# Rows normalised while they are centred, the bias added by TensorE, and a unit's sums divided on ScalarE in a graph attention kernel

## The chip, the core and the metric

The kernel runs on one core of a Trainium2 chip. The metric is device time in microseconds (us), the median of several runs. A core has TensorE (PE in the profile), VectorE (DVE), ScalarE (ACT), GpSimd (POOL) and SyncE (SP), each with its own instruction stream; they meet at semaphores. Transfers are issued by SyncE and GpSimd.

## What is computed

One graph attention layer over 8192 nodes, with rows of 256 numbers, a dense 8192 x 8192 matrix of edge weights of which few are above zero, and 8 heads of 32:

```python
h = relu((x - mean(x)) / sqrt(var(x) + 1e-5))
hw = (h @ W.T).reshape(n, 8, 32)
attn = s_src[:, None, :] + s_dst[None, :, :]      # (hw * a_src).sum(-1), (hw * a_dst).sum(-1)
attn = attn + adj[:, :, None] * We[:, 0] + be
attn = leaky_relu(where(adj[:, :, None] > 0, attn, -inf), 0.2)
attn = softmax(attn, axis=1)
out = x + einsum('ijh,jhd->ihd', attn, hw).reshape(n, 256) + h @ Wr.T + br
```

## The kernel before

**First stage.** 32 units of 256 rows. VectorE takes mean and variance of a unit (L731, L735) and the negated mean (L738). ScalarE centres and rectifies (`centre`, L1150), takes the standard deviation (`deviation`, L1154), copies the turned rows out of PSUM (`turned`, L1158) and later the projections (`copies`, L1168), scaled by one over the deviation, which VectorE makes with a reciprocal (`scales`, L743). Since the rectifier passes a positive factor, that factor is applied only behind the projections. TensorE turns the rows (`turn`, L1309) and projects them (`maps`): features and scores (L1323), and the residual `h @ Wr.T` (L1326). VectorE's `add_biases` adds `be` to the scores (L748) and makes residual times factor plus x (L753). GpSimd writes the features to a table in DRAM (L594), adds `br` to the residual (L596) and writes it to the output and to a spare copy (L600, L601). SyncE loads x into four buffers (L481). Beside this work VectorE searches the window lists: the first rows of the matrix, which have the most edges, cut into four groups of windows (L783, L772, and sorting with L841, L843). At the end the lists are ranked by length: `count` and `place` on VectorE with TensorE's sums between, ending in the ranks (L901).

**Second stage.** 67 units of 128 list rows each. Groups of lists are dealt in the order of their ranks by GpSimd (`deal`, L651) and read back (`load_dealt`, L663). For a unit of K list places GpSimd issues K gathers (L626), each of one table row per partition, into a ring of 86 slots. VectorE adds the gathered scores, applies the leaky rectifier, takes the row maximum and subtracts it (L918, L922, L926, L929). ScalarE prepares the next unit's edge terms (L1192), takes the exponentials (L1209) and weights the last two fifths of the places, head by head (L1215); VectorE weights the others (L939). TensorE sums over the places (L1347 and L1353). VectorE's `evacuate` then takes the reciprocal of the summed weights (L948) and multiplies (L952), and GpSimd adds the rows to the output four units later (L642). Between, VectorE searches the matrix rows of later units: 63 searches; one or two per unit up to unit 45, from there on one in about every second unit, and none after unit 60.

**What sets the order.** Each engine's order is written out. VectorE's unit loop is: search, then sorting steps that alternate with the four score steps, then weighting, decoding of the found list, and `evacuate` of the unit before. ScalarE's loop is: `prepare(u + 1)`, then `exps(u)`. The profile's tile names are coarse: "arena" holds the ring, the lists and all the first stage's buffers; "banks" is PSUM; "w_all" and "more_out" hold the finished rows.

## Time and profile before

| | us |
|---|---|
| median of 3 runs | 2311.83 |
| lowest and highest | 2309.43, 2316.55 |
| the profiled execution | 2312.84 |
| its span, first to last instruction | 2310.8 |

Every count of busy time and every wait is of the profiled execution. A wait is put down to what ended it. Busy shares hide which stretch an engine bounds, so the waits and the stretches are read beside them.

### The profile page before, as it was taken

How to read it: one execution, taken by the hardware profiler on the slowest of the kernel's cores; microseconds unless marked ns; L12 is line 12 of the kernel's file. 1: busy time of each engine (PE TensorE's matmuls, PEld its weight loads, DVE VectorE, ACT ScalarE, POOL GpSimd, SP SyncE). 2: the span in 40 equal slices, each digit the busy share in tenths (PEclk: the TensorE clock that was granted, in tenths of full speed). 3: DMA queues.
4: the chain of work that ended last, by engine and by line, in shares of the span. 5: the costliest groups of instructions: out<-in, count | busy, mean ns of one | idle time of the engine just before them, and what ended most of it. 6: DMA issues, size and time to landing. Idle time of an engine off the chain costs nothing. (4 is left out here: it accounts for less than half of the span.)

```text
span 2310.8 us, 22965 instructions
## 1 busy us (share of the span) xinstructions
PE 1002.1 (43%) x3773; PEld 789.3 (34%) x3774; DVE 2024.3 (88%) x5351; ACT 1115.5 (48%) x4803; POOL 1595.9 (69%) x2020
## 2 busy tenths in 40 slices
PE   4767304522453194236332643353253336363343
PEld 3555203322432173225321532242242225242232
DVE  5899797899699789999888999999999998887942
ACT  2333205633574384446543654545354446485553
POOL 5544476777776777677777777777677774777775
PEclk9998656766675667667765766666666667676676
DMA  6444876667466757877777777777778885667333
GB/s 148 161 148 138 290 229 160 200 213 236 131 212 213 223 159 235 251 236 228 219 218 222 225 254 229 249 250 247 247 256 242 257 249 174 203 197 217 88 76 65
DMA packets 164570, 473.62 MB, mean 205 GB/s; under 512 B 35888, under 2 KB 54360, under 8 KB 164216
## 3 DMA queue, kind: packets, MB, share of 16 engines
q1 hardware_dynamic: 86088, 278.11, 36.6%
q0 software_dynamic: 78336, 194.09, 30.6%
q14 instruction: 118, 0.97, 0.1%
q8 instruction: 28, 0.46, 0.1%
HBM read 435.24 MB, written 36.83 MB: 204 GB/s over the span
## 5 line engine op out<-in xcount | busy, mean ns | idle before, releaser
L626 POOL DMA_INDIRECT arena<-table,arena x1262 | 1270.7, 1007 | 479.2 <-issue 322.1
L1347 PE MATMUL banks<-arena,ident 128*128 128x264 f32 x1566 | 500.2, 492 | 1161.9 <-DVE arena L939 1161.9
L1215 ACT ACTIVATE arena<-arena 128x32 f32<-128x32 f32 x3832 | 819.3, 307 | 2.2
L1347 PEld LDWEIGHTS banks<-arena,ident 128*128 128x128 f32 x1566 | 385.0, 251 | 1273.7 <-issue 1050.9
L772 DVE FIND_INDEX8 work<-work,adj_sb 128x8 uint32<-128x502 f32 (+56 forms) x775 | 667.2, 865 | 0.0
L783 DVE MAX8 work<-adj_sb 128x8 f32<-128x502 f32 (+56 forms) x775 | 652.4, 856 | 0.0
L1209 ACT ACTIVATE arena<-pre 128x104 f32<-128x104 f32 (+22 forms) x81 | 23.3, 304 | 910.1 <-DVE pre L929 909.6
L1353 PE MATMUL banks<-arena,ident 128*128 128x264 f32 x958 | 254.4, 408 | 42.5 <-ACT arena L1215 42.5
L939 DVE TENSOR_TENSOR arena<-arena 128x1024 f32<-128x1024 f32 (+8 forms) x169 | 226.4, 1389 | 51.3 <-ACT arena L1209 51.2
L1353 PEld LDWEIGHTS banks<-arena,ident 128*128 128x128 f32 x958 | 181.7, 197 | 103.6 <-ACT arena L1215 76.2
L1192 ACT ACTIVATE pre<-arena,we_all 128x13 f32<-128x13 f32 (+26 forms) x536 | 165.3, 406 | 87.3 <-DMA arena<-lists 87.0
L918 DVE TENSOR_TENSOR pre<-pre,arena 128x104 f32<-128x104 f32 (+22 forms) x81 | 21.4, 279 | 139.2 <-DMA arena<-table,arena 129.0
L841 DVE MAX8 work<-work 128x8 f32<-128x56 f32 (+11 forms) x536 | 122.5, 270 | 2.4
L843 DVE MATCH_REPLACE8 work<-work 128x56 f32<-128x56 f32 (+11 forms) x402 | 106.6, 273 | 0.0
L642 POOL DMA_INDIRECT out_dram<-w_all,arena x41 | 66.7, 1626 | 50.2 <-DVE w_all L952 27.3
L1150 ACT ACTIVATE arena<-arena 128x256 f32<-128x256 f32 x64 | 29.0, 500 | 138.2 <-DVE arena L738 138.2
L651 POOL DMA_INDIRECT lists<-arena,rank x67 | 67.9, 1014 | 30.0 <-issue 25.0
L1323 PE MATMUL banks<-w_all,arena 128*128 128x272 f32 x256 | 83.2, 454 | 1.9 <-ACT arena L1158 1.8
L1369 PE MATMUL banks<-work,ones 128*128 128x24 f32 (+9 forms) x390 | 73.5, 336 | 0.0
L1326 PE MATMUL banks<-w_all,arena 128*128 128x256 f32 x256 | 72.3, 408 | 0.0
L596 POOL TENSOR_TENSOR arena<-arena 128x512 f32<-128x512 f32 x32 | 40.5, 1265 | 44.5 <-DVE arena L753 44.0
L1369 PEld LDWEIGHTS banks<-work,ones 128*128 128x128 f32 x390 | 69.2, 264 | 0.0
(130 smaller groups left out, 966.2 us busy)
## 6 DMA issues: line engine op xcount, KB each, us to landing
adj_sb<-in_adj_dram SPq DMA_DIRECT2D x505, 512.0 KB, 4.4
arena<-table,arena POOLq DMA_INDIRECT x1262, 3.8
table<-arena POOLq DMA_DIRECT2D x32, 264.0 KB, 2.7
arena<-in_x_dram SPq DMA_DIRECT2D x32, 256.0 KB, 2.9
resid<-arena POOLq DMA_DIRECT2D x32, 256.0 KB, 2.6
out_dram<-arena POOLq DMA_DIRECT2D x32, 256.0 KB, 2.8
adj_sb<-in_adj_dram SPq DMA_DIRECT2D x1, 1536.0 KB, 23.5
lists<-arena,rank POOLq DMA_INDIRECT x67, 3.9
```

Source lines behind the costliest of these rows:

```text
L626: pool.indirect_dma_start(gath[0:n, un.slot(k), :], None, table[:, :], bass.IndirectOffsetOnAxis(ap=rec[0:n, k, 0:1], axis=0)).then_inc(la ...
L772: v.max_index(idx8[:, 8 * s:8 * s + 8], val8[:, 8 * s:8 * s + 8], a[:, bounds[s]:bounds[s + 1]]).then_inc(S["scanned"], 1)
L783: v.max(val8[:, 8 * s:8 * s + 8], a[:, bounds[s]:bounds[s + 1]]).then_inc(S["maxed"], 1)
L841: v.max(top, keys_of).then_inc(done, 1)
L843: v.match_replace(keys_of, top, keys_of, 0.0).then_inc(done, 1)
L939: last = v.tensor_tensor(gv, gv, pb.unsqueeze(3).to_broadcast([P, n, H, D]), ALU.mult)
L1192: last = s.activation(pv[:, h, :], pairs(rec, K)[:, :, 1], ACT.Identity, scale=we_all[:, h:h + 1], bias=rec[:, 1 + h:2 + h])
L1215: last = s.activation(g, g, ACT.Copy, scale=gath[:, un.slot(k), HD + h:HD + h + 1])
L1323: m.matmul(ps_hd[:, q, b, :], rows, w_all[:, c, 0:272], start=(c == 0), stop=(c == 1))
L1347: last = m.matmul(ps_sum[:, u % 2, :], ident[:, :], gath[:, un.slot(k), :], start=(k == 0), stop=False)
L1353: last = m.matmul(ps_sum[:, u % 2, :], ident[:, :], gath[:, un.slot(k), :], start=False, stop=(k == K - 1))
L1369: m.matmul(rv[:, i, :], ones[:, :], same[:, j * D:(j + 1) * D], start=False, stop=(i == n - 1 and j == i - 1))
```

## The change

**First stage.** VectorE no longer negates the mean at once. One unit later, once ScalarE has the deviation, it takes the reciprocal and makes minus mean times reciprocal, and ScalarE normalises in the same instruction that rectifies. The projections then need no factor: ScalarE copies a unit's two blocks in one instruction, and VectorE adds residual and x in one instruction. `br` comes from TensorE, as a product of a row of ones and the row of `br`, accumulated with the residual. `add_biases` follows three units behind instead of two; x has eight buffers instead of four. GpSimd waits for its output writes after it has dealt and loaded the window lists, not before.

**Second stage.** VectorE keeps the reciprocal (`invert`), now between the score steps of the next unit and its weighting. The multiplication is on ScalarE, one instruction per head, between the exponentials and the weighting of the next unit.

```diff
-        x_sb = part(4 * 2 * IN).rearrange("p (u b n) -> p u b n", u=4, b=2)
+        x_sb = part(8 * 2 * IN).rearrange("p (u b n) -> p u b n", u=8, b=2)
...
-                    nc.gpsimd.tensor_tensor(rt_sb[:, q, :, :], rt_sb[:, q, :, :],
-                                            br_all.unsqueeze(1).to_broadcast([P, 2, HD]), ALU.add
-                                            ).then_inc(S["br_added"], 1)
-                    pool.wait_ge(S["br_added"], u + 1)
...
-            for b in range(2):
-                for q, each in (("hd_out", 16), ("res_out", 32)):
-                    pool.wait_ge(S[f"{q}{b}"], each * (UNITS // 2))
-
-            pool.wait_ge(S["pad_out"], 16)
...
             deal(groups[0])
             load_dealt(groups[0])
+            for b in range(2):
+                for q, each in (("hd_out", 16), ("res_out", 32)):
+                    pool.wait_ge(S[f"{q}{b}"], each * (UNITS // 2))
+            pool.wait_ge(S["pad_out"], 16)
...
-                dve.wait_ge(S["mv_done"], u + 1)
-                v.tensor_scalar(nmean[:, q, :], mv[:, q, :, 0], -1.0, None, ALU.mult).then_inc(S["nmean_done"], 1)
...
+                v.scalar_tensor_tensor(out=nmean[:, q, :], in0=mv[:, q, :, 0], scalar=-1.0, in1=rstd[:, q, :],
+                                       op0=ALU.mult, op1=ALU.mult).then_inc(S["nmean_done"], 1)
...
-                for b in range(2):
-                    last = v.scalar_tensor_tensor(out=rt_sb[:, q % 2, b, :], in0=ps_res[:, q % 2, b, :],
-                                                  scalar=rstd[:, q, b:b + 1], in1=x_sb[:, q, b, :],
-                                                  op0=ALU.mult, op1=ALU.add)
-                last.then_inc(S["res_done"], 1)
+                v.tensor_tensor(rt_sb[:, q % 2, :, :], ps_res[:, q % 2, :, :], x_sb[:, u % 8, :, :], ALU.add
+                                ).then_inc(S["res_done"], 1)
...
-            def evacuate(un):
+            def invert(un):
...
-                v.tensor_tensor(out_sb[u % OUTS].rearrange("p (h d) -> p h d", d=D),
-                                ps_sum[:, u % 2, 0:HD].rearrange("p (h d) -> p h d", d=D),
-                                rinv[:, u % 2, :].unsqueeze(2).to_broadcast([P, H, D]), ALU.mult).then_inc(S["evac"], 1)
...
+                    if m == 4 and un.u:
+                        invert(units[un.u - 1])
...
+                if u:
+                    evacuate(units[u - 1])
                 act.wait_ge(S["exped"], u + 1)
...
+            def evacuate(un):
+
+                u = un.u
+                act.wait_ge(S["recip"], u + 1)
+                if u >= OUTS:
+                    landed(act, units[u - OUTS].store_seq + (2 if units[u - OUTS].partial else 1))
+                for h in range(H):
+                    last = s.activation(out_sb[u % OUTS][:, h * D:(h + 1) * D], ps_sum[:, u % 2, h * D:(h + 1) * D],
+                                        ACT.Copy, scale=rinv[:, u % 2, h:h + 1])
+                last.then_inc(S["evac"], 1)
...
+                m.matmul(ps_res[:, q, :, :], ones[0:1, :], br_all[0:1, :].unsqueeze(1).to_broadcast([1, 2, HD]),
+                         start=True, stop=False)
```

Line numbers of the changed kernel differ; the names tell what is what. On TensorE, the last unit of the first stage and the ranks behind it, before:

```order
L1323 MATMUL banks<-w_all,arena 128x272 x2
L1326 MATMUL banks<-w_all,arena 128x256 x2
L1323 MATMUL banks<-w_all,arena 128x272 x2
L1326 MATMUL banks<-w_all,arena 128x256 x2
L1364 MATMUL banks<-above_sum,ones 128x61
```

The same place in the changed kernel:

```order
L1323 MATMUL banks<-arena,ones 128x512
L1328 MATMUL banks<-w_all,arena 128x272 x2
L1331 MATMUL banks<-w_all,arena 128x256 x2
L1328 MATMUL banks<-w_all,arena 128x272 x2
L1331 MATMUL banks<-w_all,arena 128x256 x2
L1370 MATMUL banks<-above_sum,ones 128x61
```

The product for `br` stands ahead of each unit's eight others, 32 times in all. On ScalarE, from the exponentials of unit 48 (128x9x8) to the weighting of unit 49, before:

```order
L1209 ACTIVATE arena<-pre 128x9x8
L1215 ACTIVATE arena<-arena 128x32 x24
L1192 ACTIVATE pre<-arena,we_all 128x7 x8
L1199 ACTIVATE pre<-ones 32x16
L1199 ACTIVATE pre<-ones 32x8
L1209 ACTIVATE arena<-pre 128x8x8
L1215 ACTIVATE arena<-arena 128x32 x24
```

The same place in the changed kernel, with the division of units 47 and 48 at L1215:

```order
L1197 ACTIVATE arena<-pre 128x9x8
L1215 ACTIVATE more_out<-banks,rinv 128x32 x8
L1205 ACTIVATE arena<-arena 128x32 x24
L1180 ACTIVATE pre<-arena,we_all 128x7 x8
L1187 ACTIVATE pre<-ones 32x16
L1187 ACTIVATE pre<-ones 32x8
L1197 ACTIVATE arena<-pre 128x8x8
L1215 ACTIVATE w_all<-banks,rinv 128x32 x8
L1205 ACTIVATE arena<-arena 128x32 x24
```

Eight instructions stand between a unit's exponentials and its weighting, ahead of everything that ScalarE does for the next unit. On VectorE, the end of unit 48 and the start of unit 49, before:

```order
L929 TENSOR_TENSOR pre<-pre,rmax 128x72
L841 MAX work<-work 128x8 x2
L834 TENSOR_SCALAR ahi<-work 128x20
L939 TENSOR_TENSOR arena<-arena 128x3x256 x2
L855 TENSOR_SCALAR arena<-work 128x20
L856 SCALAR_TENSOR_TENSOR arena<-work,ahi 128x20
L860 TENSOR_TENSOR flags<-flag,work 128x1
L948 RECIPROCAL rinv<-banks 128x8
L952 TENSOR_TENSOR more_out<-banks,rinv 128x256
L918 TENSOR_TENSOR pre<-pre,arena 128x64
```

The same place in the changed kernel:

```order
L920 TENSOR_TENSOR pre<-pre,rmax 128x72
L832 MAX work<-work 128x8 x2
L939 RECIPROCAL rinv<-banks 128x8
L825 TENSOR_SCALAR ahi<-work 128x20
L930 TENSOR_TENSOR arena<-arena 128x3x256 x2
L846 TENSOR_SCALAR arena<-work 128x20
L847 SCALAR_TENSOR_TENSOR arena<-work,ahi 128x20
L851 TENSOR_TENSOR flags<-flag,work 128x1
L909 TENSOR_TENSOR pre<-pre,arena 128x64
```

The reciprocal has moved ahead of the weighting (L939 before, L930 now), behind the score step that releases ScalarE, and the multiplication is gone.

## Rows read from the trace of the kernel before

**Rows 1.** the page, part 1: busy us, share of the span, instructions

```profile
PE 1002.1 (43%) x3773; PEld 789.3 (34%) x3774; DVE 2024.3 (88%) x5351; ACT 1115.5 (48%) x4803; POOL 1595.9 (69%) x2020
```

**Rows 2.** waits of VectorE, whole run: us in total, times, longest

```profile
DVE pre L918 <- DMA arena<-table,arena: 129.0, 16, 18.9
DVE arena L939 <- ACT arena L1209: 51.2, 16, 9.4
DVE arena L731 <- DMA arena<-in_x_dram: 10.1, 2, 5.1
DVE s_all L748 <- ACT arena L1168: 9.6, 9, 3.1
```

**Rows 3.** busy times by stretch: length, busy us per engine, granted clock, DMA

```profile
27.00:234.00 207.00, 147.00 (x578) 112.66 (x579) 182.07 (x929) 70.08 (x177) 94.37 (x110) 0.89 0.51 153
234.00:257.00 23.00, 17.99 (x89) 14.54 (x87) 11.29 (x37) 6.87 (x17) 16.45 (x19) 0.94 0.93 336
...
1477.00:1942.00 465.00, 198.27 (x752) 161.41 (x752) 459.44 (x971) 223.00 (x984) 324.95 (x316) 0.66 0.79 247
```

**Rows 4.** groups of VectorE instructions, 0-400 us: busy us, mean ns

```profile
L753 DVE SCALAR_TENSOR_TENSOR arena<-banks,arena 128x256 f32<-128x256 f32 x64 | 27.8, 476 | 1.0 <-DMA out_dram<-arena 1.0
...
L738 DVE TENSOR_SCALAR arena<-arena 128x2 f32<-128x2 f32 x32 | 9.3, 290 | 1.1
```

**Rows 5.** timeline inside the first stage: start us, us, engine, line, operation

```profile
120.23 0.76 DVE L731 BATCH_NORM_STATS2 arena<-arena 128x6 f32<-128x256 f32 x2
...
121.30 0.53 DVE L738 TENSOR_SCALAR arena<-arena 128x2 f32<-128x2 f32 x1
...
122.83 0.66 PE L1309 MATMUL banks<-ident,arena 128*128 128x128 f32 x4 [0.61 <-ACT arena L1150]
...
125.58 0.76 DVE L731 BATCH_NORM_STATS2 arena<-arena 128x6 f32<-128x256 f32 x2
...
126.30 1.03 PE L1326 MATMUL banks<-w_all,arena 128*128 128x256 f32 x4
...
138.30 0.17 DVE L738 TENSOR_SCALAR arena<-arena 128x2 f32<-128x2 f32 x1
```

**Rows 6.** the loads of x (L481): us from issue to landing

```profile
DMA to landing us min/median/max: 2.5/2.9/10.3
```

**Rows 7.** timeline of VectorE, then of GpSimd, from the window lists' ranks on

```profile
256.80 0.17 DVE L901 CAST rank<-rank_f 128x4 uint32<-128x4 f32 x1
...
264.50 1.08 POOL L651 DMA_INDIRECT lists<-arena,rank  x1 [7.71 <-issue]
...
272.85 0.80 POOL L663 DMA_DIRECT2D arena<-lists  x1 [3.46 <-DMA lists<-arena,rank]
281.11 1.15 POOL L626 DMA_INDIRECT arena<-table,arena  x1 [7.46 <-DMA arena<-lists]
```

**Rows 8.** waits of VectorE between 1942 and 2160 us

```profile
DVE arena L939 <- ACT arena L1209: 34.7, 8, 5.9
```

**Rows 9.** timeline of units 60 and 61, to the last group's deal

```profile
2190.66 6.89 ACT L1215 ACTIVATE arena<-arena 128x32 f32<-128x32 f32 x32
...
2192.92 0.20 DVE L948 RECIPROCAL rinv<-banks 128x8 f32<-128x8 f32 x1
...
2193.59 0.16 DVE L874 COPY arena<-ids 128x4 uint32<-128x4 uint32 x1
...
2204.30 0.42 DVE L901 CAST rank<-rank_f 128x4 uint32<-128x4 f32 x1
...
2206.40 0.99 POOL L651 DMA_INDIRECT lists<-arena,rank  x1 [1.14 <-DMA arena<-table,arena]
```

**Rows 10.** waits of ScalarE, then of GpSimd, whole run

```profile
ACT arena L1209 <- DVE pre L929: 909.6, 57, 84.1
...
POOL arena L626 <- PE banks L1353: 0.3, 1, 0.3
```

**Rows 11.** timeline at the end of the last unit

```profile
2293.81 0.42 DVE L952 TENSOR_TENSOR w_all<-banks,rinv 128x256 f32<-128x256 f32 x1
```

More of the change, by code:

```diff
@@ L478, in load_x @@
             def load_x(u):
[L479 to L481 removed]
+                if u >= 8:
+                    sp.wait_ge(S["x_free"], u - 7)
+                sp.dma_start(x_sb[:, u % 8, :, :], by_unit(x, u)).then_inc(S[f"x_in{u % 8}"], 16)
             for u in range(4):
@@ L727, in normalize @@
             def normalize(u, q):
-                dve.wait_ge(S[f"x_in{q}"], 16 * (u // 4) + 16)
+                dve.wait_ge(S[f"x_in{u % 8}"], 16 * (u // 8) + 16)
                 for b in range(2):
-                    last = v.bn_stats(stat[:, q, b, :], x_sb[:, q, b, :])
+                    last = v.bn_stats(stat[:, q, b, :], x_sb[:, u % 8, b, :])
                 last.then_inc(S["bn_done"], 1)
@@ L948, in evacuate @@
                 v.reciprocal(rinv[:, u % 2, :], ps_sum[:, u % 2, HD:ROW]).then_inc(S["recip"], 1)
-                if u >= OUTS:
-                    landed(dve, units[u - OUTS].store_seq + (2 if units[u - OUTS].partial else 1))
-                dve.wait_ge(S["recip"], u + 1)
-                v.tensor_tensor(out_sb[u % OUTS].rearrange("p (h d) -> p h d", d=D),
-                                ps_sum[:, u % 2, 0:HD].rearrange("p (h d) -> p h d", d=D),
-                                rinv[:, u % 2, :].unsqueeze(2).to_broadcast([P, H, D]), ALU.mult).then_inc(S["evac"], 1)
             def combine_clear():
@@ L1011, in _ @@
                 normalize(u, u % 4)
+                if u:
+                    scales(u - 1, (u - 1) % 4)
                 windows_beside(u)
-                scales(u, u % 4)
-                if u >= 2:
-                    add_biases(u - 2, (u - 2) % 4)
+                if u >= 3:
+                    add_biases(u - 3, (u - 3) % 4)
+            scales(UNITS - 1, 3)
+            count(groups[0])
+            add_biases(UNITS - 3, 1)
             add_biases(UNITS - 2, 2)
-            count(groups[0])
             add_biases(UNITS - 1, 3)
@@ L1042, in _ @@
                     done_finds += 1
-                if un.u:
-                    evacuate(units[un.u - 1])
                 for group in groups[1:]:
@@ L1055, in _ @@
                     combine_out()
-            evacuate(units[-1])
+            invert(units[-1])
             dve.wait_ge(S["fl_t"], 1)
@@ L1149, in centre @@
                 for b in range(2):
-                    last = s.activation(hn[:, q % 2, b, :], x_sb[:, q, b, :], ACT.Relu, bias=nmean[:, q, b:b + 1])
+                    last = s.activation(hn[:, q % 2, b, :], x_sb[:, u % 8, b, :], ACT.Relu, bias=nmean[:, q, b:b + 1],
+                                        scale=rstd[:, q, b:b + 1])
                 last.then_inc(S["hn_done"], 1)
             def deviation(u, q):
+                act.wait_ge(S["mv_done"], u + 1)
                 s.activation(sdev[:, q, :], mv[:, q, :, 1], ACT.Sqrt, bias=eps[:, :]).then_inc(S["sd_done"], 1)
@@ L1165, in copies @@
                     act.wait_ge(S["s_done"], u - 1)
-                act.wait_ge(S["rstd_done"], u + 1)
-                for b in range(2):
-                    last = s.activation(hd_sb[:, q % 2, b, :], ps_hd[:, q % 2, b, :], ACT.Copy,
-                                        scale=rstd[:, q, b:b + 1])
-                last.then_inc(S["hd_copied"], 1)
+                s.activation(hd_sb[:, q % 2, :, :], ps_hd[:, q % 2, :, :], ACT.Copy).then_inc(S["hd_copied"], 1)
+            deviation(0, 0)
             for u in range(UNITS):
+                if u + 1 < UNITS:
+                    deviation(u + 1, (u + 1) % 4)
                 centre(u, u % 4)
-                deviation(u, u % 4)
                 if u:
@@ L1225, in _ @@
                     s.activation(comb_w, comb_w, ACT.Exp).then_inc(S["comb_exp"], 1)
+            evacuate(units[-1])
             done = act.alloc_register("dense_act")
@@ L1302, in _ @@
             pe.wait_ge(S["wt_copied"], 2)
+            pe.wait_ge(S["small_in"], 48)
             def turn(u, q):
@@ L1325, in maps @@
                         rows = hnT[:, q, b, c * P:(c + 1) * P]
-                        last = m.matmul(ps_res[:, q, b, :], rows, w_all[:, c, 272:528], start=(c == 0), stop=(c == 1))
+                        last = m.matmul(ps_res[:, q, b, :], rows, w_all[:, c, 272:528], start=False,
+                                        stop=(b == 1 and c == 1))
                 last.then_inc(S["proj_done"], 1)
```

10 lines of the change are left out of this document (4 added, 6 removed).

## The prediction

> **What bounds the kernel now.** I read the page's busy shares first: VectorE is busy 88% of the span, ScalarE 48%, GpSimd 69% [rows 1]. A mean like that hides changes of regime, so the next views are the waits of VectorE over the whole span and the busy times by stretch. In the waits [rows 2] the reader is to see three releasers: gathered rows that have not landed (129.0 us, 16 times), ScalarE's exponentials (51.2 us, 16 times), and small waits of the first stage. With their places in the timeline they cut the run into five stretches.
>
> *0 to 257 us, the first stage and the ranks of the window lists.* VectorE is busy 182 of 207 us in its main part, TensorE 147 [rows 3]: 6.1 and 4.9 us per unit of 256 rows, thirty units. GpSimd then waits 7.7 us before it deals the window lists, though their ranks are written at 256.97 [rows 7].
>
> *281 to about 1477 us.* Most of the long gather waits lie in here, up to unit 20 at 1294 (the others are at the end); unit 27, another of the units with many places, finds its rows just landed. GpSimd issues gathers nearly without a pause, so this stretch starts and ends with the first gather at 281.11 [rows 7].
>
> *1477 to 1942 us, units 27 to 44.* VectorE is busy 459 of 465 us [rows 3]: every instruction it loses shortens the run.
>
> *1942 to 2160 us.* Units without a search of their own alternate with units that have one. VectorE waits 34.7 us for ScalarE in 8 waits [rows 8]; seven, of 2.6 to 5.9 us, are in units 46, 47, 49, 51, 53, 55 and 57. ScalarE is on the path there: it weights the rows of the unit before, prepares the next, and only then takes the exponentials.
>
> *2160 us to the end.* The last group is dealt as soon as VectorE has ranked it [rows 9], then gathers bound units 63 to 66, then the last unit's chain.
>
> **The change part by part.**
>
> *The wait for the output writes* moves behind the dealing and loading of the window lists. 7.7 us before the first deal become about 0.9, an estimate for the wake-up after a release: -6.8. The writes must still land before the first gather, but that waits longer anyway, for the loaded lists (8 us later, [rows 7]).
>
> *VectorE in the first stage.* Two operations of 476 ns [rows 4], 0.87 us together, become one over 512 elements. None such stands in the trace: it costs 0.87 if nothing is saved, about 0.70 if only a second start is; I take 0.70, since the copies from PSUM grow by about 1 ns per element. The negated mean averages 290 ns, but ran 530 while GpSimd's bias addition ran and 170 otherwise [rows 4, 5]; that addition goes, -0.12. The new order hides one dependency and adds another (the negated mean now waits for the reciprocal), about -0.08. Together -0.37 per unit, -9.6 over units 4 to 29; bounds -5 and -12.
>
> *Loads and waits.* Unit 4 waits 5.1 us for its x, unit 8 another 5.0 (the 10.1 of [rows 2]). With eight buffers x of unit 8 comes in time: -5.0. Unit 4's load is issued some 14 us earlier, but behind the window loads of the same queue; its landing took 10.3 us against a median of 2.9 [rows 6], so it comes little sooner. I take -2 (0 to -4); what is gained before unit 4 is lost in that wait. Short waits for ScalarE, counted in 9.6 us [rows 2], give -1.6 in the middle; the rest lies before unit 4 or in the tail.
>
> *TensorE* gets one product per unit, one row of ones against 512 columns. Two 256-column products beside it take 1.03 us [rows 5] at the granted 2.4 GHz, so it costs 1.03; bounds 0.5 (a single row is cheaper) and 2.1 (the lower clock). A unit took TensorE 4.5 us in [rows 5] (122.83 to 127.33); it will take 5.55. Eight of the units 5 to 29 pass VectorE in 4.7 to 5.3 us, as the 5.35 between the two L731 rows of [rows 5]. With only two buffers between the engines these become TensorE's 5.55 and keep nothing from the long units: +7.4. VectorE reaches unit 30 earlier by 2+5.0+1.6+9.6-7.4 = 10.8.
>
> *The tail of the first stage* grows. The unit behind which centring, turning and projecting run is one deeper, so at unit 30 TensorE owes four projections of 4.9 us instead of three of 3.85, then the ranks. Following the chain, the ranks are done 30.1 us after unit 30 begins, against 22.9 now: +7.2. It counts in full. The first gather moves by -6.8-10.8+7.2 = -10.4.
>
> *281 to 1477*: 0. ScalarE's later weighting frees gather slots later, but a slot is filled again some three units on, and GpSimd waits 0.3 us in the whole run for the sums of ScalarE's part [rows 10]. VectorE's savings end in its waits for gathers.
>
> *The division moved to ScalarE.* VectorE loses the time from 2192.92 to 2193.59, 0.67 us, and pays 0.13 for the reciprocal elsewhere [rows 9]: 18 units times 0.55 = -9.9 in 1477 to 1942 (8.6 to 10.4). The reciprocal comes after the step that releases the exponentials, so they don't wait for it.
>
> On ScalarE eight multiplications of 32 elements go in between exponentials and weighting. The 32 weightings of one unit take 6.89 us [rows 9], 0.215 each, so 1.72; with the reciprocal to wait for, 1.85. Read from PSUM they could cost 2.5 if they behaved like the two-operand forms. In units whose exponentials VectorE does not wait for, this is hidden by ScalarE's idle time: 909.6 us of waiting for VectorE in 57 waits [rows 10]. In the seven units named it is not: 6x1.85+1.7 = 12.8, less seven times the 0.67 that VectorE drops behind the weighting: +8.1. Units 59 and 61 become late in the same way, +2.05-0.65 and +1.55-0.65; 1.4 of slack stands before the deal of the last group [rows 9]. So +9.0; bounds +6 and +14. What is queued behind ScalarE's new wait is its own weighting, then TensorE's sums; GpSimd's stores come four units later and have time.
>
> *The last unit.* Its weighting starts 1.7 later, and its own division is 8 operations, 1.8 us, in place of 0.42 [rows 11]: +3.1.
>
> Here a rule stands against the change. The rows say that ScalarE has room in most units [rows 10] and lacks it in nine. The Trainium skill (ScalarE: Activation LUTs, Rules for kernel authors) would leave multiplications to VectorE rather than ScalarE. By the rule the move would lose wherever it is made; by the rows only where ScalarE is waited for.
>
> **Sum:** -10.4-9.9+9.0+3.1 = -8.2 against the profiled execution's 2312.84 us (2310.8 of span, 2.0 around it): 2304.6. The runs' median is 2311.83, 1.0 lower; on it the sum gives **2304** us, -0.35%. A measurement of this kernel can tell about 0.3%, 6.9 us, from no change.
>
> **The rivals.**
>
> *A larger gain.* The stage's short units cost less because TensorE's product is nearer 0.5 us (+3 in place of +7.4, a tail 2 shorter), and the lists load faster once the writes before them thin out (8 us to landing now, up to -5). For it: the first lists are among the largest and load in the busiest stretch of DMA. Against it: dealing now runs beside those writes. About -18: 2294.
>
> *The gain is eaten.* The divisions cost 2.5 us in the nine waited-for units and the tail is +4.4; the first stage gives only the 6.8 of the wait. Then -6.8-9.9+14+4.4 = +1.7: 2313.
>
> *Slower: TensorE bounds the first stage.* If the product comes at the lower clock (2.1 us) or the unit otherwise takes over 6.9 us, the pace of the thirty units now (207 over 30, [rows 3]), the stage is longer than before. At 7.2, that is 30x0.3 = +9 and +8 more for the tail, with -6.8 for the writes: the first gather is 10 later, and the rest adds -9.9+12.1: +12, 2324. For it: the granted clock is 0.89 of full there now [rows 3]. Against it: TensorE will idle less, and from 234 to 257, where it idles least, the clock is 0.94.
>
> *ScalarE is waited for in every unit.* Its new work then shows in each of the 67: 67x(1.85-0.67) = +79, 2391. The 57 waits [rows 10] speak against it. This is what the rule cited above would make of the move.
>
> *It does not do what it says:* the first stage is no shorter, and only the write wait goes. That is -6.8-9.9+12.1 = -4.6, 2307, inside the forecast's range.
>
> **How the numbers follow.** Forecast (2299 to 2309) 0.42; larger gain 0.18; eaten 0.26; slower 0.13; ScalarE in every unit 0.01. The threshold, 2304.9, halves the forecast and leaves the larger gain whole: faster 0.21+0.18 and a part of luck in the eaten case, 0.43; same 0.42; slower 0.15. The range reaches from the larger gain to the middle of the slower case: 2292 to 2318. The forecast's own is 2299 to 2309.
>
> **What would show it.** In the profile after: the first gather near 271; TensorE's units in the first stage 5.5 us apart where they were 4.7 to 5.3, and four of them back to back at its end; no bias addition on GpSimd, and a negated mean near 170 ns; VectorE's waits for exponentials up from 51 to about 65 us with the same nine units; 18 units between 1477 and 1942 shorter by 0.55 each; first-list deal within 1 us of the ranks. Wrong would be a first gather later than 278 or before 262, ScalarE's eight divisions over 2.2 us, or a wait of VectorE on the sums at the reciprocal's new place.

## The result: 0.9% faster, more than forecast

The changed kernel takes 2295.82 us (median of 7 runs, 2288.58 to 2297.49); the kernel before, on the same chip, 2316.55 us (7 runs, 2309.43 to 2324.84). The ratio is 0.9909, with a 95% interval of 0.9893 to 0.9925. That is 21 us, where the forecast had 8. Its sign was right and the time lies in the stated range, but it lies outside the forecast's own range, next to the rival that was called a larger gain.

The profiled execution of the changed kernel has a span of 2295.8 us against 2310.8. The page's busy shares, which answer to [rows 1]:

```profile
PE 1064.3 (46%) x3837; PEld 806.6 (35%) x3838; DVE 1980.8 (86%) x5252; ACT 1205.9 (53%) x5306; POOL 1551.3 (68%) x1988
```

VectorE lost 43.5 us of work, ScalarE gained 90, GpSimd lost its 40 us of additions, TensorE gained 62. The waits of VectorE over the whole span, which answer to [rows 2] (us in total, times, longest):

```profile
DVE pre L909 <- DMA arena<-table,arena: 142.6, 17, 20.0
DVE rinv L939 <- PE banks L1359: 47.7, 10, 5.9
DVE s_all L742 <- ACT arena L1156: 30.3, 14, 6.9
DVE arena L930 <- ACT arena L1197: 26.9, 16, 7.2
...
DVE arena L725 <- DMA arena<-in_x_dram: 4.8, 1, 4.8
```

Two things are new. The waits for x fell from two to one. And the wait for ScalarE's exponentials fell from 51.2 to 26.9 us, while a wait of 47.7 us stands at the reciprocal (L939), for TensorE's sums. Both are one wait cut in two: in a unit without a search VectorE now comes first to the reciprocal of the unit before, whose sums wait for ScalarE's weighting, and then to the exponentials, which come out of ScalarE a little later. Together they are 74.6 us; the forecast had about 65.

Set against the terms of the forecast, with a second profile of the same kernel (e8 below):

| stretch | forecast | changed kernel | second profile |
|---|---|---|---|
| first gather | -10.4 | 281.1 to 266.6: -14.5 | -13.8 |
| first gather to unit 27's scores | 0 | 1195.8 to 1203.5: +7.7 | -1.6 |
| units 27 to 44 | -9.9 | 465.5 to 453.7: -11.9 | -11.8 |
| unit 45 to the deal of the last group | +9.0 | 263.9 to 269.0: +5.1 | +5.1 |
| from there to the end of the span | +3.1 | 104.4 to 103.1: -1.4 | -0.4 |
| sum | -8.2 | -15.0 | -22.5 |

Four of five terms repeat within 1 us in the second profile. The second stretch does not: it differs by 9 us between two executions of one kernel, and the profile that came with the result was the slowest of its seven runs (2297.49 us). The rows from the ranks of the window lists on answer to [rows 7] (timeline of VectorE, then of GpSimd: start us, us, engine, line, operation, idle time before and what ended it):

```profile
253.88 0.16 DVE L892 CAST rank<-rank_f 128x4 uint32<-128x4 f32 x1
...
254.34 1.07 POOL L641 DMA_INDIRECT lists<-arena,rank  x1 [1.86 <-DVE rank L892]
...
261.38 0.80 POOL L653 DMA_DIRECT2D arena<-lists  x1 [2.15 <-DMA lists<-arena,rank]
266.63 1.00 POOL L616 DMA_INDIRECT arena<-table,arena  x1 [4.45 <-issue]
```

The ranks come 2.9 us earlier (the forecast: 3.6). GpSimd deals 0.3 us behind them instead of 7.5. Two savings were not forecast: dealing takes 7.0 us instead of 8.4, and from the loading of the lists to the first gather it takes 5.3 us instead of 8.3.

### The profile page after: what moved, and what is told of

The parts are those of the page before. It is cut to its first block and busy times, and to the rows that moved or that the text cites. A ratio compares the mean times of both kernels' runs of the same rounds, so it can differ in the third digit from the quotient of the medians.

```text
span 2295.8 us, 23433 instructions
## 1 busy us (share of the span) xinstructions
PE 1064.3 (46%) x3837; PEld 806.6 (35%) x3838; DVE 1980.8 (86%) x5252; ACT 1205.9 (53%) x5306; POOL 1551.3 (68%) x1988
## 5 line engine op out<-in xcount | busy, mean ns | idle before, releaser
L1353 PE MATMUL banks<-arena,ident 128*128 128x264 f32 x1566 | 507.9, 497 | 1082.2 <-DVE arena L930 1042.6
L1353 PEld LDWEIGHTS banks<-arena,ident 128*128 128x128 f32 x1566 | 390.2, 254 | 1196.4 <-issue 739.7
L1359 PE MATMUL banks<-arena,ident 128*128 128x264 f32 x958 | 271.4, 417 | 77.2 <-ACT arena L1205 76.8
L930 DVE TENSOR_TENSOR arena<-arena 128x1024 f32<-128x1024 f32 (+8 forms) x169 | 226.5, 1390 | 27.0 <-ACT arena L1197 26.9
L593 POOL DMA_DIRECT2D table<-arena x32 | 22.9, 717 | 105.0 <-ACT arena L1156 101.3
L1375 PE MATMUL banks<-work,ones 128*128 128x24 f32 (+9 forms) x390 | 79.9, 355 | 0.0
L1375 PEld LDWEIGHTS banks<-work,ones 128*128 128x128 f32 x390 | 75.8, 287 | 0.0
L1215 ACT ACTIVATE w_all<-banks,rinv 128x32 f32<-128x32 f32 x360 | 68.9, 302 | 3.3 <-DVE rinv L939 2.0
```

The lines of the kernel that those rows point to most:

```text
L930: last = v.tensor_tensor(gv, gv, pb.unsqueeze(3).to_broadcast([P, n, H, D]), ALU.mult)
L1353: last = m.matmul(ps_sum[:, u % 2, :], ident[:, :], gath[:, un.slot(k), :], start=(k == 0), stop=False)
L1359: last = m.matmul(ps_sum[:, u % 2, :], ident[:, :], gath[:, un.slot(k), :], start=False, stop=(k == K - 1))
L1375: m.matmul(rv[:, i, :], ones[:, :], same[:, j * D:(j + 1) * D], start=False, stop=(i == n - 1 and j == i - 1))
```

## The experiments

Ratios are to the kernel before on the same chip, with 95% intervals. The numbers of the profiles are times from the start of the span.

**The two halves apart.** e1 keeps the changed first stage and gives the whole division back to VectorE (parts of its edit):

```diff
+        def on_act(v):
+            return False
...
-                    if m == 4 and un.u:
+                    if m == 4 and un.u and on_act(un.u - 1):
                         invert(units[un.u - 1])
...
+                if un.u and not on_act(un.u - 1):
+                    evacuate(units[un.u - 1])
...
-                if u:
+                if u and on_act(u - 1):
                     evacuate(units[u - 1])
```

`on_act(v)` says whether ScalarE divides unit v; the added `evacuate` is VectorE's reciprocal and multiplication.

> The changed first stage alone: the reciprocal and the multiplication by it stay on VectorE, in one place behind the decoding, as before; everything up to the first gather is as in the changed kernel. Two theories about the 7.7 us that the changed kernel loses between its first gather (14.5 us earlier than before) and unit 27 (6.8 us earlier). Theory A, the divisions on ScalarE delay the weighting and with it the gather slots: here the stretch from the first gather to the scores of unit 27 takes 1196 us as before, unit 27 comes 14.5 us earlier, and the kernel ends about 14 us earlier than before (ratio 0.994). Theory B, the stretch hangs on how long gathers take to land, which differs from one execution to the next and with the phase of the window loads: it takes 1196 to 1204 us here too, unit 27 comes 7 to 14 us earlier, ratio 0.994 to 0.997. For both: nothing more is won between units 27 and 44 (0 where the changed kernel wins 11.9) and nothing lost behind unit 45 (0 where it loses 6.3 by unit 60).

Measured: 2298.66 us, ratio 0.9928 (0.9911 to 0.9944). First gather at 267.1, unit 27 at 1463.4 (stretch 1196.4), then 465.3 us to unit 45, as before (465.5), and 265.4 to the last deal (263.9 before). So the first stage alone brings about 0.7%.

e2 is the kernel before with the opposite half: reciprocal ahead of the weighting, eight multiplications on ScalarE.

> The kernel before with the division alone moved to ScalarE and the reciprocal ahead of the weighting. First gather at 281 us as before. Theory A (slots freed later): unit 27 comes 5 to 8 us later than before. Theory B: within 4 us of before, either way. Both: units 27 to 44 win 11 to 12 us (18 times 0.66, as in the changed kernel), the units without a search and the last deal give back 5 to 7, so the ratio is 0.996 to 0.998 by theory B and about 1.000 by theory A.

Measured: 2306.1 us, ratio 0.9956 (0.9939 to 0.9973). First gather 281.4; units 27 to 44 take 453.3 us, 12.3 less than before; unit 45 to the last deal 269.0, 5.1 more. The division alone is worth about 0.4%, and its gain and its loss stand where the forecast put them. Its stretch up to unit 27 took 1204.3 us, which looked like theory A; the ratio is nearer to theory B's. The two halves add to 1.2%, where the whole change has 0.9%; their intervals just allow it.

**What the stretch up to unit 27 hangs on.** e8 is the changed kernel again.

> The changed kernel once more, for a second profile. Theory A (divisions on ScalarE delay slots): the stretch from the first gather to the scores of unit 27 takes 1203 to 1205 us again. Theory B (it differs from one execution to the next): it may take 1195 to 1204; 1198 or less would show it.

Measured: 2289.95 us in one run; the stretch took 1194.3 us, with the same divisions on ScalarE as in the profile with 1203.5. So the divisions alone do not make it slow, and theory A falls as it was put. GpSimd's pauses of over 0.3 us between the first gather and unit 27's (what each idle time there has over 0.3, summed) come to 78.7 us in the slower profile of the changed kernel and 72.9 in this one; what most of them wait for is a gather four before its own, since four transfers may be under way. e7 takes that limit away:

```diff
-LANES = 4
+LANES = 8
```

> The changed kernel with eight transfers under way at once instead of four on GpSimd's queue (a gather waits until the one eight before it has landed). In six profiles so far the stretch from the first gather to the scores of unit 27 took 1195.6 to 1196.4 us three times and 1203.5 to 1204.3 three times, and GpSimd's pauses of over 0.3 us in it come to 70 and to 78 us. Theory B (these pauses are waits for the landing of the gather four before, and their sum differs from one execution to the next): most of the 70 to 78 us go, GpSimd's part of the stretch falls by 30 to 60 us, VectorE's searches bound part of it, unit 27 comes 20 to 45 us earlier, the kernel is 1 to 2% faster than the changed one and its executions lie closer together. Theory C (the transfers themselves are the limit, more of them under way only land later): the stretch stays at 1195 to 1204 us.

Measured: 2259.28 us (2256.60 to 2261.05), ratio 0.9755 (0.9738 to 0.9772), the stretch 1154.7 us, the pauses 19.4. GpSimd's waits from the first gather to unit 27's, in the changed kernel and then in e7 (us in total, times, longest):

```profile
POOL arena L616 <- issue: 196.4, 618, 4.5
POOL arena L616 <- DMA arena<-table,arena: 75.1, 120, 2.7
```

```profile
POOL arena L616 <- issue: 226.1, 705, 7.3
POOL arena L616 <- DMA arena<-table,arena: 13.7, 45, 0.3
```

In the first fence 120 pauses wait for a landing, up to 2.7 us; in the second no such pause is over 0.3, the usual step between two gathers. The transfers still land 4.1 us after their issue (median) in both, and yet 40 to 49 us are gone: the limit was the count under way, not the transfers. The 4.4 us between the lowest and highest of its runs, against 8.9 of the changed kernel, fit theory B as well. Which transfers collide to make one execution slower by 9 us was not traced.

**The write wait.** e3 puts it back ahead of the deal:

```diff
+            for b in range(2):
+                for q, each in (("hd_out", 16), ("res_out", 32)):
+                    pool.wait_ge(S[f"{q}{b}"], each * (UNITS // 2))
+            pool.wait_ge(S["pad_out"], 16)
             deal(groups[0])
             load_dealt(groups[0])
-            for b in range(2):
-                for q, each in (("hd_out", 16), ("res_out", 32)):
-                    pool.wait_ge(S[f"{q}{b}"], each * (UNITS // 2))
-            pool.wait_ge(S["pad_out"], 16)
```

> The changed kernel with GpSimd's wait for the output writes back ahead of the dealing of the window lists. The forecast priced this wait at 6.8 us. Theory A, that price still holds in the changed kernel: the first gather at 273 to 274 us instead of 266.6, and 4 to 7 us of it are left at the end. Theory B, in the changed kernel the last writes leave earlier against the ranks (the last one is issued 1.6 us before the ranks are there and a write takes 3.5 us to land), so the wait costs 2 to 3 us and the first gather is at 269. The time from the loading of the lists to the first gather, 5.2 us in the changed kernel and 8.3 before, shows whether the quicker load belongs to the order of wait and deal (then 8 here) or not (then 5).

Measured: 2299.32 us, ratio 0.9924 (0.9906 to 0.9942); the interval overlaps with that of the changed kernel. In the profile:

```profile
255.56 0.17 DVE L892 CAST rank<-rank_f 128x4 uint32<-128x4 f32 x1
...
257.70 1.07 POOL L641 DMA_INDIRECT lists<-arena,rank  x1 [3.54 <-issue]
...
266.33 0.80 POOL L653 DMA_DIRECT2D arena<-lists  x1 [3.74 <-DMA lists<-arena,rank]
271.28 1.00 POOL L616 DMA_INDIRECT arena<-table,arena  x1 [4.15 <-DMA arena<-lists]
```

With the wait ahead of the deal, GpSimd stands 2.0 us behind the ranks, not 7.5, and the lists still load in 5.0 us, not 8.3. Theory B holds on both counts: most of the 7.5 us had gone by another way. The first gather, at 271.3, lies between the two theories (269, and 273 to 274): of the 4.7 us by which it is later than in the changed kernel, 1.7 stand at the wait, 1.7 came with later ranks and 1.6 went into dealing (8.6 us instead of 7.0), which neither theory had; the lists loaded 0.3 faster.

**The ring of eight alone.** e6 is the kernel before with eight buffers for x.

```diff
-                if u >= 4:
-                    sp.wait_ge(S["x_free"], u - 3)
-                sp.dma_start(x_sb[:, u % 4, :, :], by_unit(x, u)).then_inc(S[f"x_in{u % 4}"], 16)
+                if u >= 8:
+                    sp.wait_ge(S["x_free"], u - 7)
+                sp.dma_start(x_sb[:, u % 8, :, :], by_unit(x, u)).then_inc(S[f"x_in{u % 8}"], 16)
```

> The kernel before with eight buffers for x instead of four, and nothing else. The forecast gave this 5.0 us at unit 8 and 2 (0 to 4) at unit 4. Theory A: VectorE waits for x once (unit 4, 3 to 5 us) instead of twice, the 5.0 at unit 8 are kept up to unit 30, which begins at 227 to 229 instead of 234.1. Theory B: what is won at unit 8 is lost again in waits for ScalarE's copies (TensorE is only 5 us behind there), and unit 30 begins at 231 to 234.

Measured, one run: 2304.11 us beside a median of 2317.24. VectorE waits for x once (4.2 us); unit 30 begins at 228.8, 5.3 us earlier (theory A). But the first gather is at 268.1, 13.0 us earlier, with the write wait and all the arithmetic as they were:

```profile
252.12 0.16 DVE L901 CAST rank<-rank_f 128x4 uint32<-128x4 f32 x1
...
253.86 1.08 POOL L651 DMA_INDIRECT lists<-arena,rank  x1 [3.06 <-issue]
...
262.66 0.80 POOL L663 DMA_DIRECT2D arena<-lists  x1 [3.91 <-DMA lists<-arena,rank]
268.14 1.00 POOL L626 DMA_INDIRECT arena<-table,arena  x1 [4.68 <-DMA arena<-lists]
```

Why is to be read from SyncE's queue. Behind the last load of x it holds the matrix rows for VectorE's next searches. The last x load and the first of these rows, in the kernel before, the changed one and e6 (first issue, us to the last, line, count):

```profile
173.26 61.12 SPq L481 DMA_DIRECT2D arena<-in_x_dram  x9
234.42 49.19 SPq L510 DMA_DIRECT2D adj_sb<-in_adj_dram  x21
```

```profile
174.21 30.10 SPq L481 DMA_DIRECT2D arena<-in_x_dram  x5
204.36 74.36 SPq L510 DMA_DIRECT2D adj_sb<-in_adj_dram  x24
```

```profile
176.34 19.84 SPq L481 DMA_DIRECT2D arena<-in_x_dram  x4
196.23 81.23 SPq L510 DMA_DIRECT2D adj_sb<-in_adj_dram  x24
```

With four buffers the last load of x waits for a unit near the end, and the matrix rows start at 234, in the 23 us in which the last output writes leave. With eight they start at 204 (changed kernel) or 196 (e6). Busy times by stretch (length, busy us of each engine, granted clock, DMA share, GB/s), first before, then changed:

```profile
210.00:234.00 24.00, 16.30 (x54) 12.47 (x55) 23.03 (x89) 6.98 (x18) 10.29 (x12) 0.79 0.40 132
...
257.00:285.00 28.00, 0.00 (x0) 0.00 (x0) 27.86 (x120) 3.88 (x12) 7.85 (x8) 0.50 0.80 264
```

```profile
210.00:234.00 24.00, 23.15 (x86) 16.41 (x85) 18.13 (x71) 9.14 (x20) 7.83 (x11) 0.87 0.96 337
234.00:257.00 23.00, 18.23 (x85) 13.38 (x84) 9.48 (x53) 4.23 (x8) 10.60 (x14) 0.93 0.74 262
257.00:285.00 28.00, 0.00 (x0) 0.00 (x0) 27.90 (x102) 6.73 (x17) 16.41 (x17) 0.50 0.74 229
```

The burst of 336 GB/s stood between 234 and 257 [rows 3]; now it stands between 210 and 234, and the writes and the lists behind it find room. The last writes to the output (issues from 246 to 262 us, their count, size, median us to landing) show it directly, first before, then e6:

```profile
out_dram<-arena POOLq DMA_DIRECT2D x3, 256.0 KB, 5.8
```

```profile
out_dram<-arena POOLq DMA_DIRECT2D x2, 256.0 KB, 2.8
```

They land 5.8 us after their issue beside the burst and 2.8 behind it (3.0 in the changed kernel): the rows that SyncE loads delay the writes that GpSimd issued. The Trainium skill (DMA: Bandwidth & Descriptors, Issuing engines are not separate DMA queues) says that transfers issued by different engines run on the same 16 DMA engines and interleave; these rows agree.

Of e6's 13.0 us, 4.7 stand at the ranks, where what was won at unit 8 arrives; 5.9 are the shorter wait for the writes and 2.8 the faster loading of the lists, less 0.4 for dealing. The whole changed first stage brings the first gather 14.5 us (13.8 in the second profile). So on top of the ring, normalising while centring, TensorE's product and the moved wait together are worth 0.8 to 1.5 us there, which single profiles can't tell from nothing.

**TensorE's product.** e5 leaves it out, and `br` with it.

```diff
-                m.matmul(ps_res[:, q, :, :], ones[0:1, :], br_all[0:1, :].unsqueeze(1).to_broadcast([1, 2, HD]),
-                         start=True, stop=False)
```

> The changed kernel with TensorE's product of ones and br left out (br is not added at all). It prices the product: it takes 1.02 us per unit from start to start in the changed kernel, where units follow each other 5.25 us apart at the short units and back to back at the end of the first stage. Theory A (the forecast: the product bounds the short units, eight of them, and the tail): the ranks of the window lists come 3 to 4 us earlier for the tail and 3 to 7 more for the short units, 244 to 248 instead of 254.0. Theory B (VectorE and the searches set the pace up to unit 30 and only the tail is TensorE's): unit 30 begins at 225 to 226 as in the changed kernel, and the ranks come 3 to 4 us earlier, near 250.

Measured, one run: 2284.01 us; unit 30 at 219.2 (225.6 with the product), ranks at 243.0 (254.0), first gather at 255.5 (266.6). That is theory A, and 1 us more than it: the product costs 6.4 us up to unit 30 and 4.6 in the tail. e9 lets GpSimd add `br` again instead:

```diff
+                    nc.gpsimd.tensor_tensor(rt_sb[:, q, :, :], rt_sb[:, q, :, :],
+                                            br_all.unsqueeze(1).to_broadcast([P, 2, HD]), ALU.add
+                                            ).then_inc(S["br_added"], 1)
+                    pool.wait_ge(S["br_added"], u + 1)
```

> The changed kernel with the addition of br undone: GpSimd adds br again (1.27 us per unit) and TensorE's product is gone. Without product and without any addition of br the ranks came at 243.0 us instead of 254.0 and the first gather at 255.5 instead of 266.6. Theory: the product costs the first stage more than it saves, since GpSimd has time there; the ranks come at 243 to 247, the first gather at 256 to 260, and the kernel ends 7 to 10 us before the changed one (ratio to the kernel before 0.986 to 0.988). Rival: with the addition back, the negated mean is slow beside it again (0.5 us instead of 0.17) and the output writes of the last units leave 2 us later, so that the ranks come at 249 or later and the ratio stays within 0.990 to 0.991.

Measured: 2292.59 us, ratio 0.9907 (0.9877 to 0.9937), no different from the changed kernel. The ranks come 6.1 us earlier, at 247.9, but the first gather only 1.9, at 264.7: the negated mean takes 336 ns again instead of 162, GpSimd deals 2.4 us behind the ranks, and dealing takes 8.6 us instead of 7.0. My theory was right up to the ranks and wrong behind them. It is a draw between the two places.

**Who should divide.** e4 lets ScalarE divide only where its next exponentials are not waited for:

```diff
+        def on_act(v):
+            return v + 2 < len(units) and found[v + 2] > found[v + 1]
```

> The changed kernel with a rule for who divides: ScalarE divides unit v only where unit v+2 has a search (its own next exponentials are then not waited for), VectorE divides the others, behind the decoding as before. Theory: the loss of 6.3 us between units 45 and 60 and the 1.1 us of the last unit are ScalarE's 1.37 us of divisions on the path in nine units, so they go, while VectorE keeps its savings in units with a search: unit 60 comes 18 to 24 us earlier than before where the changed kernel has 12.4, and the kernel ends 7 to 10 us before the changed one (ratio to the kernel before 0.986 to 0.988). Rival: the last group's deal or the gathers at the end bound it, then unit 63 comes no more than 2 us earlier than in the changed kernel and the ratio stays 0.990 to 0.991.

Measured: 2295.28 us, ratio 0.9913 (0.9893 to 0.9933): no gain that a measurement tells. In the profile units 45 to 60 take 244.6 us, 7.8 less than in the changed kernel, as expected. But the last group's ranks now come while GpSimd is still issuing gathers:

```profile
2175.47 0.17 DVE L896 CAST rank<-rank_f 128x4 uint32<-128x4 f32 x1
...
2174.52 0.87 POOL L620 DMA_INDIRECT arena<-table,arena  x1 [0.31 <-issue]
2177.51 1.63 POOL L636 DMA_INDIRECT out_dram<-more_out,arena  x1 [2.11 <-DMA arena<-table,arena]
2179.65 0.99 POOL L645 DMA_INDIRECT lists<-arena,rank  x1 [0.52 <-issue]
```

4.0 us pass from the ranks to the deal (0.3 in the changed kernel), and the end of the span stands 16.3 us behind the last store instead of 14.3, so that 2 of the 7.8 are left. The rival named the place; its size was off, since from unit 45 on unit 63 comes 4.3 us earlier than in the changed kernel and not at most 2.

**Put together.** e10 joins e4 and e7; e11 adds e9.

> The changed kernel with eight transfers under way on GpSimd's queue and the rule for who divides (ScalarE where unit v+2 has a search, else VectorE). In the profile with four transfers the rule won 7.8 us between units 45 and 60, of which 3.7 were lost again because GpSimd was behind with its gathers when the last group's ranks came (4.0 us from the ranks to the deal, 0.3 without the rule). With eight under way GpSimd is ahead there. Theory: the 7.8 us are kept to the end, unit 45 to the last store takes 353 us or less (360.5 with eight transfers and no rule), ratio 0.971 to 0.973. Rival: the last deal still comes over 3 us behind the ranks, and the ratio is 0.974 or more.

> The kernel of the run before with br added by GpSimd too: eight transfers, the rule for who divides, no product on TensorE. If the three gains add, as stretches that follow each other should: first gather at 256 to 260 us instead of 268.6, the rest as in the run before, ratio 0.967 to 0.970. Rival: an earlier first gather is lost in VectorE's searches, which now bound much of the stretch up to unit 27 (no waits for gathers left to lose it in): it shifts with the stage, so no loss is expected unless units 1 to 20 take over 8 us longer.

Measured: 2295.53 us, ratio 0.9917 (0.9891 to 0.9942), and 2291.21, ratio 0.9892 (0.9866 to 0.9918). Yet in the profile of e10 all that was expected is there: the last deal 0.3 us behind the ranks, unit 45 to the last store in 350.0 us (360.5 in e7), and the last store at 2226.4 us, 14.4 earlier than in e7 (3.9 of it from before unit 45). In e11 the third gain does not add: its first gather comes at 265.0 us and not at 256 to 260, for the reasons of e9, and its last store at 2226.7. In both, the span ends 64 to 65 us behind the last store. In that time no engine computes; a program's last step reads eight flags and branches past code that is not needed here. Its branches, in e10 (durations in ns as min/median/max, first and last start in us), and what the DMA queues carried from 2227 us on:

```profile
L413 DVEq COMPARE_BRANCH  x8: 56/56/72, 2228.3 to 2237.8; - x8
L413 ACTq COMPARE_BRANCH  x8: 45/45/45, 2228.4 to 2287.4; - x8
```

```profile
q14 instruction: 38, 0.31, 1.7%
```

VectorE does its eight rounds in 9.5 us, ScalarE in 59: some 45 us pass between its branches and the instructions that follow them, and 13 behind the reading of the flags. e7 carried 3 instruction transfers in the same place, e10 38. e12 is e11 with waits that are long satisfied put into ScalarE's program, which move all that follows by 64 instructions:

```diff
+            for _ in range(128):
+                act.wait_ge(S["hd_copied"], UNITS)
             prepare(units[0])
```

> The kernel of e11 with 128 waits that are already satisfied put into ScalarE's program behind the first stage, where it idles: they do nothing but move what follows by 64 instructions. In the two kernels with eight transfers and the rule the last store leaves at 2226.4 and 2226.7 us, and yet the span ends at 2290.5 and 2291.7, since ScalarE takes 45 us over the branches of its last loop (the loop over the eight groups of flags, whose body is skipped) where it takes 6 to 7.5 in all other kernels; 30 instruction transfers go with it where the others have 3. Theory: where this loop lies in the program decides it, nothing else; shifted, it takes 6 to 8 us again, the span ends 14 to 16 us behind the last store, near 2242, and the ratio to the kernel before is 0.966 to 0.970. Rival: it hangs on what ScalarE did before (fewer divisions), then the 45 us stay.

Measured: 2246.36 us (2243.21 to 2247.91), ratio 0.9708 (0.9692 to 0.9724). ScalarE's branches take 7.0 us, 3 instruction transfers are carried, and the span ends 16.5 us behind the last store. So the place decides it, and not the fewer divisions; why that one place is slow is not shown. This is the fastest kernel here, 2.9% before the kernel before and 2.0% before the changed one:

```profile
q14 instruction: 3, 0.02, 0.4%
```

## Why the prediction was right in sign and short in size

**The write wait, -6.8.** The number was right by luck (7.5 to 0.3 us), the cause was not. I priced the move behind the deal. With the wait moved back (e3) GpSimd is 2.0 us behind the ranks; with the ring alone and the wait in place (e6) it is 1.6. The failed step is in the part on loads: I followed what x's own loads gain from eight buffers and did not ask what stands behind them in SyncE's queue. The rows that I read there, a DMA share of 0.93 and 336 GB/s from 234 to 257 [rows 3], were the cause of the wait, in plain sight.

**The lists, 0.** For the same reason the lists load in 5.3 us, not 8.3. I had put that into a rival ("up to -5, once the writes before them thin out") and not into the sum. Dealing itself took 1.3 less; it takes 7.0 us where GpSimd comes to it from a wait for the ranks (the changed kernel, e1, e8) and 8.6 to 8.8 in e3, e6 and e9, where it comes to it later. Why is open.

**Unit 30, -10.8; measured -8.4 and, in the second profile, -9.5.** The wait at unit 8 went as forecast (5.0 us). The one at unit 4 stayed at 4.8, so nothing of the 2 came. The addition over 512 elements takes 683 ns where I took 700, and the negated mean 162 where I took 170. TensorE's product takes 1.02 us from start to start, and short units follow each other 5.25 us apart (5.55 forecast). I had priced the product by the duration of two others, 1.03 us; from start to start such a pair takes 0.86. What VectorE saved came to 0.2 us per unit between units 10 and 30, not 0.37: its waits for ScalarE's copies rose from 9.6 to 30.3 us, where I had let them fall by 1.6. Without the product (e5) they are 16.4 us and the saving is 0.38. So VectorE's saving was priced rightly, and the product took about half of it.

**The tail, +7.2; measured +5.5 and +7.2.** Right within the 2 us by which the two profiles differ, and e5 shows the price of the choice: the whole product costs 11.0 us at the ranks, where the sum implied 7.4 and some 4 in the tail.

**281 to 1477 us, 0.** Not refuted, and not shown to the last us: ten profiles with four transfers under way have 1194.3 to 1204.3 us. The seven in which ScalarE divides in this stretch average 1200.0, the three in which VectorE does 1197.0 (1195.8 before). So few profiles do not exclude that the divisions cost a few us here. That one execution can differ from the next by 9 us in this stretch I had not seen, and it is as large as the whole sum.

**18 units, -9.9; measured -11.9.** 0.66 us per unit instead of 0.55 (0.67 less 0.13 is 0.54). I charged the 0.13 for the reciprocal. In its new place it costs nothing: between the end of the score step that releases ScalarE and the start of the weighting VectorE has to wait for the exponentials anyway, 0.37 us (median of the 18 units) with the reciprocal there and without it. A unit of this stretch before, then one in the changed kernel:

```profile
1506.70 0.29 DVE L929 TENSOR_TENSOR pre<-pre,rmax 128x136 f32<-128x136 f32 x1
...
1507.37 3.16 DVE L939 TENSOR_TENSOR arena<-arena 128x1280 f32<-128x1280 f32 x2
```

```profile
1526.33 0.28 DVE L920 TENSOR_TENSOR pre<-pre,rmax 128x120 f32<-128x120 f32 x1
...
1526.77 0.19 DVE L939 RECIPROCAL rinv<-banks 128x8 f32<-128x8 f32 x1
...
1526.97 2.63 DVE L930 TENSOR_TENSOR arena<-arena 128x1024 f32<-128x1024 f32 x2
```

**The units that wait for ScalarE, +9.0; measured +5.1** (+3.6 against e1, where VectorE divides behind the same first stage). The mechanism and the units were right (e4 takes 7.8 us out of units 45 to 60, where most of them lie); the price of the eight divisions was too high. In units 60 and 61:

```profile
2178.32 1.54 ACT L1215 ACTIVATE more_out<-banks,rinv 128x32 f32<-128x32 f32 x8
...
2179.69 6.90 ACT L1205 ACTIVATE arena<-arena 128x32 f32<-128x32 f32 x32
```

From the first division to the first weighting 1.37 us pass, 0.171 each, where I had taken the 0.215 of the weightings and a wait for the reciprocal, 1.85. That reciprocal was waited for 3 times in the run, 2.0 us in all. The sign of what would have shown me wrong came up here: VectorE does wait for sums at the reciprocal's new place, 35.0 us in seven waits between 1924 and 2143. It costs nothing, since the exponentials for which it would wait next come later still (another 13.4 us in eight waits).

**The last unit, +3.1; measured -0.9 and, in the second profile, -0.1** (from its scores to the end of the span). The step that failed is what the end hangs on. I followed the last store, which indeed comes 1.1 us later against the unit's scores. But the span ends with the loop over the flags, which waits for VectorE: in all profiles but those of e10 and e11 the end stands 15.0 to 15.7 us behind VectorE's last step for the flags (L1063 before, L1051 in the changed kernel), whoever divides. The first of these steps (L1059, L1047) stood behind VectorE's multiplication; now it stands behind the reciprocal:

```profile
2294.16 0.27 DVE L1059 TENSOR_REDUCE flagT<-banks 64x1 f32<-64x128 f32 x1
```

```profile
2279.48 0.21 DVE L939 RECIPROCAL rinv<-banks 128x8 f32<-128x8 f32 x1 [4.62 <-PE banks L1359]
2279.61 0.27 DVE L1047 TENSOR_REDUCE flagT<-banks 64x1 f32<-64x128 f32 x1
```

It comes 7.64 us behind the unit's scores instead of 8.13 (8.22 in the second profile; 7.9 against 8.5 on average over seven profiles each, with the last division on ScalarE or on VectorE). So the end stands 14.1 to 14.7 us behind the last store in the kernels where ScalarE divides last and 16.0 to 16.5 where VectorE does, again without e10 and e11.

**The rivals.** The larger gain had the time almost right (2294) and half its reason: the lists did load faster, but the product cost 1.02 us, not 0.5. The gain was not eaten: eight divisions cost 1.37 us, not 2.5. The first stage is shorter (unit 30 8.4 us earlier, the ranks 2.9), so the change does what it says. TensorE did not bound the whole stage: 5.25 us per short unit against the 6.9 from which it would have. ScalarE was not waited for in every unit. The rule of the Trainium skill that stood against the change (ScalarE: Activation LUTs, Rules for kernel authors: multiply on VectorE rather than on ScalarE) does not hold here as a whole: VectorE is the faster one at it (0.42 us against 1.37), and yet moving the division alone brought 0.44% (e2). It holds where ScalarE is waited for (e4).

## What to carry to other kernels

When a ring of buffers gets deeper, ask what stands behind its loads in their queue: here 8 of the ring's 13 us came from later transfers that moved out of the way of the stage's end, and 5 from the loads themselves. Before costing an edit in a stretch that gathers bound, read what a gather waits for: where it is the landing of the one four before, a deeper window is worth more here (1.5%, 36 us by the ratios) than all the arithmetic around it. When an engine divides or copies for another, decide it unit by unit: give it the work in units whose next result nobody waits for.

## What the runs showed of the hardware

ScalarE's multiplications of 128x32 elements out of PSUM into SBUF follow each other 0.171 us apart, those from SBUF to SBUF 0.215; I had expected PSUM to be no faster. TensorE's product of one row against 512 columns takes 1.02 us from start to start, no less than two products of 128 rows against 256 columns beside it (0.86).

The place of a loop in an engine's program can cost 2%. ScalarE's last loop, whose body is skipped, spends 6 to 7.5 us on its branches, up to the instruction behind each, in eleven profiles, and about 45 in the two of e10 and e11, where its program is of the same length; 64 instructions further on (e12) it takes 7.0. In e10 all branches but the last are followed by 2.7 to 4.2 us until the next instruction, where in the other kernels only the first is (2.6 to 3.9) and the rest by 0.2; the queue that loads instructions is busy meanwhile, with 38 transfers instead of 3. The Trainium skill (Advanced Engine Details and Errata, Control Flow Timing) gives about 108 ns for a compare-and-branch; the branches here take 45 to 214 ns (median, by engine), and the 2.7 to 4.2 us behind them stand outside of that figure.
